# Rotating q and k with the other half of the partitions, in a kernel of windowed attention and routed experts

## Chip, cores and metric

The kernel runs on one core of a Trainium2 chip. The metric is the time of one execution on the device in microseconds (us). The engines are called as the profile calls them: PE (TensorE, matrix products), PEld (its loads of weights), DVE (VectorE), ACT (ScalarE), POOL (GpSimd), SP (SyncE, whose queue issues most of the DMAs).

## What is computed

One transformer layer over 16 batches of 256 tokens of width 128, with 16 heads of 8 dimensions. Cut to what matters here:

```python
q = (layernorm(x) @ q_w.T + q_b)            # per head: (B, H, S, 8)
k = (ctx @ k_w.T + k_b)
def apply_rope(x):                          # half = 4
    x1, x2 = x[..., :half], x[..., half:]
    return concatenate([x1 * cos - x2 * sin, x1 * sin + x2 * cos], axis=-1)
q, k = apply_rope(q) * d ** -0.5, apply_rope(k)
# each query looks at its own key and the 64 before it
probs = softmax(q . k over the window);  x = x + (probs . v) @ o_w.T + o_b
# then: layernorm, top 2 of 8 experts with limited capacity, silu(h @ w1) @ w2, weighted sum
```

A head's rotated vector needs, for each dimension, the dimension itself times a cosine and the one four further on (or back) times a sine.

## The kernel before

The work has two stages. The attention stage goes through the 16 batches in steps, each of which works on several batches at once: in step k the scores and probabilities of batch k, the maxima of batch k+1, the projections and the rotation of batch k+3, the first normalisation of batch k+4, and behind them the output of batch k-1 and the routing of batch k-2, whose rows POOL scatters to the queues of the experts in DRAM. The expert stage follows: 8 experts, three chunks of rows each.

Every engine has its program written out by hand in a fixed order (`body(k, par, pair)` for each engine, run from step -4 to 17, the middle ones in a loop), and the engines meet only at semaphores: `after(engine, name, per, batch)` waits until `name` has been raised `per` times for each batch so far. So an instruction that waits holds up all that stands behind it on its engine.

PE goes through eight units u in each step. In a unit stand the scores by key of batch k, the scores by query of batch k+1, one of the smaller jobs, and the products of the probabilities with v. The projections are such jobs (`project`): of q at u = 3 into bank m0, of k at u = 4 into bank m2. The normalised x and the context lie transposed in `xcT`, with the dimensions on the partitions. Weights are laid out with the outputs ordered by dimension: partition d * 16 + h holds dimension d of head h, so partitions 0 to 63 hold dimensions 0 to 3 of all heads and 64 to 127 dimensions 4 to 7. WQ and WK are the columns of these weights in `wts`, WQR and WKR the same with the halves exchanged. Each projection is made twice, side by side in one bank.

DVE adds the bias (a column of `cbias`) and multiplies with a table of `cst`: with cosines into `straight`, with signed sines into `turned` (`rope`, L989; i = 0 and 1). The rotation of q is in DVE's order between the pieces of the routing of batch k-2 (`diff`, `chosen`, `both`) and ahead of the sixth maximum of the step; that of k stands behind the two `xn` (L927, the normalisation of batch k+4) and ahead of the seventh maximum.

POOL adds both to `qk` (L1306). Then q and k are cut into three bf16 parts whose sum is the f32 value: ACT casts the first (L810), POOL takes the rest (L1309), ACT casts the second (L814), POOL makes the third (L1312). In POOL's order follow `rstd` of the second normalisation (L1316), four indirect DMAs to the queues (L1260), and in the next step `base` (L1292), the tags (L1293) and `rstd` of the first normalisation (L1298), for which DVE's `xn` wait, and then the next `qk`.

SP's queue takes the parts to scratch memory (L340, L345), from where q_pack and k_pack are loaded. Behind these it has the maxima: PE transposes them (L564), ACT copies them to `maxT` (L767), SP writes them out (L371) and reads them back into a row of q_pack (L378), and PE waits for that ahead of u = 0 and u = 4 of its scores by key. SP also loads `xres` (L407), which waits for `x1` (L1129), the residual sum on DVE. `masks` (L1060) are copies at the start of the program, on partitions 64 to 127, which stand right behind the rotation of k in the second and third step.

The pieces of the code that decide:

```python
cos, sin = np.cos(ang).astype(f), np.sin(ang).astype(f)
sin = np.where((np.arange(P) // HEADS < half)[:, None], -sin, sin)
...
a = np.concatenate([a[:, HD // 2:], a[:, :HD // 2]], axis=1)     # by_dim(w, turn=True)
```

Of the kernel before, what the change touches and what calls it, by code (L numbers as in the profile page):

```python
# [31 lines left out]
ALU = mybir.AluOpType  # L32
# [3 lines left out]
P = 128  # L36
BATCHES = 16
TOKENS = 256
CONTEXT = 1601
DIM = 128  # L40
# [39 lines left out]
WQ, WQR, WK, WKR, WV, WO, WR = (n * DIM for n in range(7))  # L80
# [3 lines left out]
def build(nc, x, ctx_in, weights, col_bias, row_bias, consts, consts16, q_rows, k_rows, w1, w2, out):  # L84
# [7 lines left out]
    with es:  # L92
# [12 lines left out]
        cst = sb("cst", [P, CONSTS])  # L105
        cst16 = sb("cst16", [P, 3 * P], BF16)
        wts = sb("wts", [P, WEIGHTS])
        cbias = sb("cbias", [P, 5])
# [19 lines left out]
        xcT = two("xcT", [P, 2 * TOKENS])  # L128
        straight = sb("straight", [P, 2, TOKENS])
        turned = sb("turned", [P, 2, TOKENS])  # L130
# [61 lines left out]
        S = {}  # L192
# [11 lines left out]
        def after(eng, name, per, batch, n=None):  # L204


            n = per if n is None else n
            if isinstance(batch, int):
                if batch >= BATCHES:
                    batch, n = BATCHES - 1, per  # L210
                if batch * per + n <= 0:
                    return
            eng.wait_ge(S[name], batch * per + n)
# [246 lines left out]
        def _(pe):  # L460
            def mm(o, l, r, start=True, stop=True):
                return nc.tensor.matmul(o, l, r, start=start, stop=stop)  # L462
# [9 lines left out]
            def readers(k, *waits):  # L472
                for name, per, batch, n in (waits if isinstance(k, int) else waits[-1:]):
                    after(pe, name, per, batch, n)

            def in_turn(n, this, before):


                return before[n:] + this[:n]

            def m0_read(k, n):
                readers(k, *in_turn(n, [("v_s", 1, k + 1, 1), ("norm_s", 2, k - 1, 1), ("roped_q", 2, k + 3, 2),
                                        ("ranked", 1, k - 2, 1)],
                                    [("v_s", 1, k, 1), ("norm_s", 2, k - 2, 1), ("roped_q", 2, k + 2, 2),
                                     ("ranked", 1, k - 3, 1)]))

            def m1_read(k, n):
# [3 lines left out]
                                     ("mt_s", 2, k, 1), ("ctxt_s", 1, k - 2, 1)]))  # L491

            def m2_read(k, n):
                readers(k, *in_turn(n, [("xn2t_s", 1, k - 2, 1), ("indexed", 2, k - 2, 2), ("roped_k", 2, k + 3, 2),
                                        ("x1_s", 1, k - 1, 1)],
                                    [("xn2t_s", 1, k - 3, 1), ("indexed", 2, k - 3, 2), ("roped_k", 2, k + 2, 2),
                                     ("x1_s", 1, k - 2, 1)]))

            def scores_by_query(j, par, u):
# [77 lines left out]
                        last = nc.tensor.transpose(m1[:, (2 + t) * P:(3 + t) * P], cin[1 - par][:, t, :], ident)  # L577
                    last.then_inc(S["xt_mm"], 1)

            def project(k, par, m, w, wr, cols, name, free, n):  # L580
                if on(k + 3):
                    free(k, n)
                    after(pe, "xct_s", 1, k + 3)
                    mm(m[:, 0:TOKENS], wts[:, w:w + DIM], xcT[1 - par][:, cols:cols + TOKENS])
                    mm(m[:, TOKENS:2 * TOKENS], wts[:, wr:wr + DIM], xcT[1 - par][:, cols:cols + TOKENS]
                       ).then_inc(S[name], 1)

            def context_across(k, par, t):
                j = k - 1
# [8 lines left out]
            def body(k, par, pair):  # L598
                if isinstance(k, int) and k == -1:
                    pe.wait_ge(S["obias_s"], 1)  # L600
                for u in range(UNITS):
                    scores_by_key(k, par, u)
                    if u < UNITS - 1:
                        scores_by_query(k + 1, 1 - par, u + 1)
                    else:
                        if isinstance(k, int) and -2 <= k < 0:
                            pe.wait_ge(S["masks_made"], 3 * (k + 3))
                        scores_by_query(k + 2, par, 0)
                    if u == 0:
                        values(k, par)  # L610
                        maxima_across(k, k, 1, 0)
                    if u == 1:
                        inputs_across(k, par)
                    if u == 2:
                        if on(k - 2):
                            m2_read(k, 0)
                            after(pe, "xn2_s", 2, k - 2)
                            for t in range(TILES):
                                last = nc.tensor.transpose(m2[:, t * P:(t + 1) * P], rows[par][:, 0, t, 0:DIM], ident)
                            last.then_inc(S["xn2t_mm"], 1)  # L620
                        context_across(k, par, 0)
                        context_across(k, par, 1)
                        if on(k - 2):
                            m2_read(k, 1)
                            for t in range(TILES):
                                last = mm(m2[:, t * EXPERTS:(t + 1) * EXPERTS], xn2T[:, t * P:(t + 1) * P],
                                          wts[:, WR:WR + EXPERTS])
                            last.then_inc(S["logit_mm"], 1)
                    if u == 3:
                        project(k, par, m0, WQ, WQR, 0, "q_mm", m0_read, 2)  # L630
                        maxima_across(k, k + 1, 0, 3)
                    if u == 4:
                        project(k, par, m2, WK, WKR, TOKENS, "k_mm", m2_read, 2)
                    if u == 5:
                        if on(k - 1):
                            m1_read(k, 4)
                            after(pe, "norm_s", 2, k - 1)
                            for t in range(TILES):
                                last = nc.tensor.transpose(m1[:, t * P:(t + 1) * P], ctxn[:, t, :], ident)
                            last.then_inc(S["ctxt_mm"], 1)  # L640
                        if on(k - 2):
                            m0_read(k, 3)
                            after(pe, "both_s", 1, k - 2)

                            b = both16[:].rearrange("p t e -> p (t e)")
                            mm(m0[:, 0:16], earlier16, b, True, False)
                            mm(m0[:, 8:16], ones16, b[:, 0:8], False, True)
                            mm(m0[:, 16:24], ones16, b[:, 0:8], True, False)
                            mm(m0[:, 16:24], ones16, b[:, 8:16], False, True).then_inc(S["prefix_mm"], 1)
                    if u == 6 and on(k - 1):  # L650
                        m2_read(k, 3)
                        after(pe, "ctxt_s", 1, k - 1)
                        if isinstance(k, int) and k == 1:
                            pe.wait_ge(S["bias_made"], 4)
                        mm(m2[:, 0:TOKENS], ones16[0:BIAS_ROWS, :], bias_rows[:].rearrange("p t c -> p (t c)"), True, False)
                        for t in range(TILES):
                            last = mm(m2[:, t * P:(t + 1) * P], ctxT[:, t * P:(t + 1) * P], wts[:, WO:WO + DIM], False, t == TILES - 1)
                        last.then_inc(S["y_mm"], 1)
                    if u == 0:
                        weigh_values(k - 1, 1 - par, UNITS - 1)  # L660
                    else:
                        weigh_values(k, par, u - 1)
# [210 lines left out]
        def _(dve):  # L873
            v = nc.vector
# [107 lines left out]
            def rope(k, name, mms, m, which, c0, b0, i):  # L982

                if not on(k + 3):
                    return
                if i == 0:
                    after(dve, mms, 1, k + 3)
                    after(dve, "qk_s", 1, k + 2)
                v.scalar_tensor_tensor((straight, turned)[i][:, which, :], m[:, i * TOKENS:(i + 1) * TOKENS],  # L989
                                       cbias[:, b0 + i:b0 + i + 1], cst[:, c0 + i * TOKENS:c0 + (i + 1) * TOKENS],  # L990
                                       ALU.add, ALU.mult).then_inc(S[name], 1)

            def route(k, par, n):

# [243 lines left out]
        def _(pool):  # L1238
# [48 lines left out]
            def body(k, par, pair):  # L1287
# [11 lines left out]
                if isinstance(k, int) and k == FIRST:  # L1299
                    start()  # L1300
                if on(k + 3):
                    after(pool, "roped_q", 2, k + 3)
                    after(pool, "roped_k", 2, k + 3)
                    after(pool, "part1", 1, k + 2)
                    after(pool, "rest_s", 1, k + 2)
                    g.tensor_tensor(qk[:], straight[:], turned[:], ALU.add).then_inc(S["qk_s"], 1)  # L1306
                    after(pool, "part1", 1, k + 3)
                    after(pool, "part2", 1, k + 2)
                    g.tensor_tensor(rest[:], qk[:], parts[:, 0, :, :], ALU.subtract).then_inc(S["rest_s"], 1)  # L1309
# [102 lines left out]
```

## Time and profile before

| | us |
|---|---|
| median of 3 runs | 570.44 (567.39 to 571.85) |
| profiled execution | 574.74 |
| its span, first to last instruction | 572.7 |
| filling the pipeline, 0 to 129.4 us of the span | 129.4 |
| attention, 129.4 to 246.3 us | 116.9 |
| last batches, routing and scatter, 246.3 to 358 us | 111.7 |
| experts, 358 us to the end | about 215 |

In the stretch from 129.4 to 246.3 us PE is busy 105.5 us, DVE 99.5, ACT 63.8 and POOL 84.4, at a granted clock of 1.00; in the expert stage PE is busy 148.9 of 215 us and POOL 139.6. A busy share says what an engine has to do, not that the others wait for it: for that one reads the gaps, what ended them, and the chain of the work that ended last. PE's busy time is modelled from the starts of its instructions, since matrix products overlap; each f32 product has two records. On POOL neighbouring records overlap too, and where the profile puts a gap down to "issue" it knows of no instruction that ended it.

### The profile page before, as it was taken

Reading aid. Unit: us, or ns where it says so; the run is one execution under the profiler, and the core shown is the slowest. Engines: PE = TensorE matmul, PEld = TensorE weight load, DVE = VectorE, ACT = ScalarE, POOL = GpSimd, SP = SyncE. Lnnn points to the kernel's source line nnn. Section 1 sums busy time; section 2 is a strip of 40 time slices with the busy share of each in tenths; the row PEclk is TensorE's granted clock in tenths of the full one; section 3 lists DMA queues with packets and bytes.
Section 4 is the critical chain, followed back from the end, with each engine's and each line's share of the span. In section 5 each row is a group of like instructions: output and inputs, shape, how many; then the busy total and the mean of one; then the engine's idle time right before and its main releaser. Section 6 shows DMA issues by size and latency. Waiting matters only on the chain.

```text
span 572.7 us, 16559 instructions
## 1 busy us (share of the span) xinstructions
PE 410.8 (72%) x5570; PEld 321.5 (56%) x5570; DVE 345.2 (60%) x1055; ACT 262.9 (46%) x578; POOL 344.1 (60%) x289
## 2 busy tenths in 40 slices
PE   3373598779988999788869830499978769879300
PEld 2252466657766776666657620378867658668200
DVE  4783376757988888868766652177635636545200
ACT  1111255435654555444444620289847748557100
POOL 6432023357776777765664677007787687787874
PEclk9995788999999999989988975599989989888855
DMA  9895766577877888876875335524554554432432
GB/s 184 210 242 146 174 191 171 148 161 164 193 155 172 184 183 174 166 163 148 153 156 106 43 51 77 138 83 67 108 83 64 106 83 60 78 32 25 36 28 18
DMA packets 89615, 70.50 MB, mean 123 GB/s; under 512 B 9632, under 2 KB 76448, under 8 KB 89056
## 3 DMA queue, kind: packets, MB, share of 16 engines
q1 hardware_dynamic: 68576, 60.36, 41.2%
q0 software_dynamic: 20992, 9.53, 19.3%
q8 instruction: 28, 0.46, 0.4%
q14 instruction: 19, 0.16, 0.1%
HBM read 39.11 MB, written 31.00 MB: 122 GB/s over the span
## 4 chain that ended last, share of the span: by engine, by line
POOL 25%; issue 18%; DMA 7%; PE 6%; SPq 3%; DVE 1%; ACT 1%; POOLq 0%; ACTq 0%; DVEq 0%
POOL out L1336 16%; POOL queues L1260 6%; PE bank L462 5%; DMA out<-ys,row_token 3%; DMA maxima_scratch<-maxT 1%; SPq L345 1%; SPq L340 1%; DMA q_pack<-maxima_scratch 1%; DMA xs<-queues 1%; POOL base L1292 1%; POOL parts L1312 1%; POOL rest L1309 1%; DMA queues<-rows,index 1%; PE bank L681 0%; ACT parts L810 0%
## 5 line engine op out<-in xcount | busy, mean ns | idle before, releaser
L1336 POOL DMA_INDIRECT out<-ys,row_token x88 | 138.8, 1578 | 68.4 <-DVE ys L1195 31.3
L885 DVE TENSOR_REDUCE maxima<-bank 128x4 f32<-128x512 f32 x128 | 87.3, 685 | 63.8 <-PE bank L462 60.6
L1260 POOL DMA_INDIRECT queues<-rows,index x64 | 100.6, 1571 | 19.8 <-issue 19.1
L753 ACT ACTIVATE probs<-bank 128x512 f32<-128x512 f32 x128 | 76.4, 597 | 78.3 <-PE bank L462 77.8
L462 PE MATMUL bank<-xTp,w1p 128*128 128x512 f32 (+1 forms) x288 | 71.6, 403 | 13.4 <-DVE xTp L1146 13.4
L462 PE MATMUL bank<-q_pack,k_pack 128*128 128x64 bf16 x1024 | 54.9, 199 | 34.3 <-DMA q_pack<-maxima_scratch 32.8
L462 PEld LDWEIGHTS bank<-xTp,w1p 128*128 128x128 f32 x288 | 53.8, 213 | 25.4 <-issue 8.3
L856 ACT ACTIVATE hid<-bank 128x512 f32<-128x512 f32 (+1 forms) x96 | 53.7, 559 | 29.6 <-PE bank L462 28.4
L462 PE MATMUL bank<-k_pack,q_pack 128*64 128x128 bf16 x1024 | 56.1, 236 | 15.6 <-DMA k_pack<-k_scratch 15.6
L462 PEld LDWEIGHTS bank<-q_pack,k_pack 128*128 128x128 bf16 x1024 | 39.1, 101 | 48.6 <-DMA q_pack<-maxima_scratch 32.5
L462 PE MATMUL bank<-probs,v_sb 128*32 128x64 f32 x2048 | 57.6, 231 | 7.8 <-ACT csb L760 4.9
L1218 DVE TENSOR_TENSOR hidp<-hid,hidp 128x512 fp32r<-128x512 f32 (+1 forms) x96 | 55.4, 601 | 12.4 <-ACT hidp L860 11.5
L462 PE MATMUL bank<-hidp,w2p 128*128 128x512 f32 (+1 forms) x288 | 61.7, 363 | 0.5 <-DVE hidp L1218 0.5
L1195 DVE TENSOR_TENSOR ys<-bank,row_gate 128x512 f32<-128x512 f32 (+1 forms) x24 | 14.4, 602 | 75.6 <-DMA out<-ys,row_token 74.6
L1306 POOL TENSOR_TENSOR qk<-straight,turned 128x512 f32<-128x512 f32 x16 | 22.2, 1390 | 58.1 <-DVE turned L989 37.9
L860 ACT ACTIVATE hidp<-bank 128x512 fp32r<-128x512 f32 (+1 forms) x96 | 54.2, 564 | 0.0
L462 PEld LDWEIGHTS bank<-hidp,w2p 128*128 128x128 f32 x288 | 46.8, 188 | 7.8 <-issue 0.8
L462 PEld LDWEIGHTS bank<-probs,v_sb 128*32 128x32 f32 x2048 | 36.5, 112 | 21.7 <-issue 12.6
L462 PEld LDWEIGHTS bank<-k_pack,q_pack 128*64 128x64 bf16 x1024 | 34.9, 116 | 24.1 <-issue 8.1
L462 PE MATMUL bank<-xcT,wts 128*128 128x256 f32 x128 | 42.9, 469 | 5.7 <-ACT xcT L784 5.7
L462 PEld LDWEIGHTS bank<-xcT,wts 128*128 128x128 f32 x128 | 25.9, 223 | 12.3 <-issue 5.9
L1298 POOL TENSOR_TENSOR rstd<-var,half_neg 128x2 f32<-128x2 f32 x16 | 16.0, 997 | 26.3 <-DVE var L922 26.2
(113 smaller groups left out, 664.6 us busy)
## 6 DMA issues: line engine op xcount, KB each, us to landing
k_pack<-k_scratch SPq DMA_DIRECT2D x64, 192.0 KB, 3.9
q_pack<-q_scratch SPq DMA_DIRECT2D x64, 128.0 KB, 3.2
queues<-empty SPq DMA_DIRECT2D x8, 682.5 KB, 7.3
xs<-queues SPq DMA_DIRECT2D x8, 650.0 KB
q_scratch<-parts SPq DMA_DIRECT2D x16, 192.0 KB
k_scratch<-parts SPq DMA_DIRECT2D x16, 192.0 KB
xin<-in_x SPq DMA_DIRECT2D x16, 128.0 KB, 3.2
cin<-in_ctx SPq DMA_DIRECT2D x16, 128.0 KB, 3.4
```

Of the source, the lines that this page charges most:

```text
L340: sp.dma_start(to[:, at:at + times, :], parts[:, part, 0, :].unsqueeze(1).to_broadcast([P, times, TOKENS])).then_inc(S["scr_w"], 16)
L462: return nc.tensor.matmul(o, l, r, start=start, stop=stop)
L753: nc.scalar.activation(probs[u % 2][:], bb[u % 2][:], ACT.Exp).then_inc(S["prob_s"], 1)
L856: nc.scalar.activation(hid[s][:, f, 0:CHUNKS[c]], up[f][:, 0:CHUNKS[c]], ACT.Silu).then_inc(S["silu_s"], 1)
L860: nc.scalar.activation(hidp[s][:, 0, f, 0:CHUNKS[c]], up[f][:, 0:CHUNKS[c]], ACT.Silu).then_inc(S["h_hi"], 1)
L885: v.reduce_max(maxima[par][:, 4 * hg:4 * hg + 4, i2], ab[u % 2][:].rearrange("p (h c) -> p h c", c=P), AX).then_inc(S["max_s"], 1)
L1195: ins = v.tensor_tensor(ys[s][:, 0:m, :], yt[:, 0:m * DIM].rearrange("p (t c) -> p t c", c=DIM), row_gate[par][:, t0:t0 + m].unsqueeze(2). ...
L1218: v.tensor_tensor(hidp[s][:, 1, f, 0:CHUNKS[c]], hid[s][:, f, 0:CHUNKS[c]], hidp[s][:, 0, f, 0:CHUNKS[c]].bitcast(F32), ALU.subtract).then ...
L1260: g.indirect_dma_start(queues, bass.IndirectOffsetOnAxis(ap=index[par][:, n:n + 1], axis=0), rows[par][:, n // TILES, n % TILES, :], None, ...
L1298: g.tensor_tensor(rstd1[:], var1[:], half_neg[:], ALU.pow).then_inc(S["rstd1_s"], 1)
L1306: g.tensor_tensor(qk[:], straight[:], turned[:], ALU.add).then_inc(S["qk_s"], 1)
L1336: g.indirect_dma_start(out, bass.IndirectOffsetOnAxis(ap=row_token[par][0:n, t:t + 1], axis=0), ys[s][0:n, col // P, :], None, compute_op= ...
```

## The change

The projections with exchanged weights go. `project` makes one product of 128x256 for q and one for k. `straight` is made as before. `turned` is made by two instructions on 64 partitions each: partitions 0 to 63 of `turned` from partitions 64 to 127 of the projection, and the other way round; bias column and table of sines are read on the partitions that are written. `roped_q` and `roped_k` are raised three times in a batch instead of twice, and those who wait for them wait for three. The columns WQR and WKR are still loaded with the weights.

```diff
@@ PE: project, and its two calls
-            def project(k, par, m, w, wr, cols, name, free, n):
+            def project(k, par, m, w, cols, name, free, n):
                 if on(k + 3):
                     free(k, n)
                     after(pe, "xct_s", 1, k + 3)
-                    mm(m[:, 0:TOKENS], wts[:, w:w + DIM], xcT[1 - par][:, cols:cols + TOKENS])
-                    mm(m[:, TOKENS:2 * TOKENS], wts[:, wr:wr + DIM], xcT[1 - par][:, cols:cols + TOKENS]
-                       ).then_inc(S[name], 1)
+                    mm(m[:, 0:TOKENS], wts[:, w:w + DIM], xcT[1 - par][:, cols:cols + TOKENS]).then_inc(S[name], 1)
@@ DVE: rope
-                v.scalar_tensor_tensor((straight, turned)[i][:, which, :], m[:, i * TOKENS:(i + 1) * TOKENS],
-                                       cbias[:, b0 + i:b0 + i + 1], cst[:, c0 + i * TOKENS:c0 + (i + 1) * TOKENS],
-                                       ALU.add, ALU.mult).then_inc(S[name], 1)
+                if i == 0:
+                    v.scalar_tensor_tensor(straight[:, which, :], m[:, 0:TOKENS], cbias[:, b0:b0 + 1],
+                                           cst[:, c0:c0 + TOKENS], ALU.add, ALU.mult).then_inc(S[name], 1)
+                else:
+                    for here, there in ((slice(0, P // 2), slice(P // 2, P)), (slice(P // 2, P), slice(0, P // 2))):
+                        v.scalar_tensor_tensor(turned[here, which, :], m[there, 0:TOKENS], cbias[here, b0 + 1:b0 + 2],
+                                               cst[here, c0 + TOKENS:c0 + 2 * TOKENS], ALU.add, ALU.mult
+                                               ).then_inc(S[name], 1)
@@ POOL: ahead of qk (PE's waits for its banks m0 and m2 alike)
-                    after(pool, "roped_q", 2, k + 3)
-                    after(pool, "roped_k", 2, k + 3)
+                    after(pool, "roped_q", 3, k + 3)
+                    after(pool, "roped_k", 3, k + 3)
```

In DVE's order of a middle step before, from the rotation of q (first straight and turned) to that of k and the maximum behind it:

```order
L989 SCALAR_TENSOR_TENSOR straight<-bank,cbias,cst 128x256
L1021 TENSOR_TENSOR diff<-top 128x2
L1023 TENSOR_TENSOR chosen<-cst,top_index 128x32
L989 SCALAR_TENSOR_TENSOR turned<-bank,cbias,cst 128x256
L1030 TENSOR_TENSOR both<-chosen 128x16
L885 TENSOR_REDUCE maxima<-bank 128x4
L927 TENSOR_SCALAR xn<-xin,mv,rstd 128x128 x2
L989 SCALAR_TENSOR_TENSOR straight<-bank,cbias,cst 128x256
L989 SCALAR_TENSOR_TENSOR turned<-bank,cbias,cst 128x256
L885 TENSOR_REDUCE maxima<-bank 128x4
```

The same place now:

```order
L988 SCALAR_TENSOR_TENSOR straight<-bank,cbias,cst 128x256
L1024 TENSOR_TENSOR diff<-top 128x2
L1026 TENSOR_TENSOR chosen<-cst,top_index 128x32
L992 SCALAR_TENSOR_TENSOR turned<-bank,cbias,cst 64x256 x2
L1033 TENSOR_TENSOR both<-chosen 128x16
L883 TENSOR_REDUCE maxima<-bank 128x4
L925 TENSOR_SCALAR xn<-xin,mv,rstd 128x128 x2
L988 SCALAR_TENSOR_TENSOR straight<-bank,cbias,cst 128x256
L992 SCALAR_TENSOR_TENSOR turned<-bank,cbias,cst 64x256 x2
L883 TENSOR_REDUCE maxima<-bank 128x4
```

Nothing has moved; each turned has become two of 64 partitions, at the place of the one.

In PE's order of a middle step before, from u = 3 (the projection of q) to u = 4 (that of k); q_pack and k_pack are the scores, max_parts the transposed maxima:

```order
L462 MATMUL bank<-xcT,wts 128x256 x2
L564 MATMUL bank<-cst,max_parts 32x128
L462 MATMUL bank<-probs,v_sb 32x64 x8
L462 MATMUL bank<-q_pack,k_pack 128x64 x8
L462 MATMUL bank<-k_pack,q_pack 64x128 x8
L462 MATMUL bank<-xcT,wts 128x256 x2
```

The same place now:

```order
L462 MATMUL bank<-xcT,wts 128x256
L564 MATMUL bank<-cst,max_parts 32x128
L462 MATMUL bank<-probs,v_sb 32x64 x8
L462 MATMUL bank<-q_pack,k_pack 128x64 x8
L462 MATMUL bank<-k_pack,q_pack 64x128 x8
L462 MATMUL bank<-xcT,wts 128x256
```

One product stands where two stood, and all else keeps its place.

## Rows read from the trace of the kernel before

**Rows 1.** The page: busy time by engine; chain that ended last.
```profile
PE 410.8 (72%) x5570; PEld 321.5 (56%) x5570; DVE 345.2 (60%) x1055; ACT 262.9 (46%) x578; POOL 344.1 (60%) x289
...
POOL 25%; issue 18%; DMA 7%; PE 6%; SPq 3%; DVE 1%; ACT 1%; POOLq 0%; ACTq 0%; DVEq 0%
```

**Rows 2.** Timeline of POOL: start, us, engine, line, form [idle before, releaser].
```profile
196.73 1.27 POOL L1306 TENSOR_TENSOR qk<-straight,turned 128x512 f32<-128x512 f32 x1 [1.56 <-issue]
198.80 1.16 POOL L1309 TENSOR_TENSOR rest<-qk,parts 128x512 f32<-128x512 f32 x1 [0.81 <-ACT parts L810]
...
202.86 1.59 POOL L1260 DMA_INDIRECT queues<-rows,index  x1 [0.21 <-issue]
...
210.25 1.28 POOL L1298 TENSOR_TENSOR rstd<-var,half_neg 128x2 f32<-128x2 f32 x1
213.09 1.27 POOL L1306 TENSOR_TENSOR qk<-straight,turned 128x512 f32<-128x512 f32 x1 [1.56 <-issue]
```

**Rows 3.** Timeline of DVE in the same step, 193 to 197 us.
```profile
193.72 0.47 DVE L989 SCALAR_TENSOR_TENSOR turned<-bank,cbias,cst 128x256 f32<-128x256 f32 x1
...
194.31 0.68 DVE L885 TENSOR_REDUCE maxima<-bank 128x4 f32<-128x512 f32 x1
195.20 0.60 DVE L927 TENSOR_SCALAR xn<-xin,mv,rstd 128x128 f32<-128x128 f32 x2 [0.22 <-POOL rstd L1298]
195.72 0.48 DVE L989 SCALAR_TENSOR_TENSOR straight<-bank,cbias,cst 128x256 f32<-128x256 f32 x1
196.11 0.47 DVE L989 SCALAR_TENSOR_TENSOR turned<-bank,cbias,cst 128x256 f32<-128x256 f32 x1
196.51 0.68 DVE L885 TENSOR_REDUCE maxima<-bank 128x4 f32<-128x512 f32 x1
```

**Rows 4.** Timeline of POOL: first and last qk of the stretch, and the next.
```profile
143.78 1.28 POOL L1298 TENSOR_TENSOR rstd<-var,half_neg 128x2 f32<-128x2 f32 x1
146.80 1.26 POOL L1306 TENSOR_TENSOR qk<-straight,turned 128x512 f32<-128x512 f32 x1 [1.75 <-issue]
...
246.33 1.27 POOL L1306 TENSOR_TENSOR qk<-straight,turned 128x512 f32<-128x512 f32 x1 [2.02 <-issue]
...
266.02 1.27 POOL L1306 TENSOR_TENSOR qk<-straight,turned 128x512 f32<-128x512 f32 x1 [4.63 <-DVE turned L989]
```

**Rows 5.** Timeline of DVE: copies on partitions 64 to 127 behind the rotation.
```profile
26.87 0.47 DVE L989 SCALAR_TENSOR_TENSOR turned<-bank,cbias,cst 128x256 f32<-128x256 f32 x1
27.38 1.22 DVE L1060 COPY q_pack<-mask_rows 64x4096 bf16<-64x4096 bf16 x1
28.52 4.38 DVE L1060 COPY k_pack<-mask_rows 64x4096 bf16<-64x4096 bf16 x2
```

**Rows 6.** All instructions of DVE by form: few partitions against many.
```profile
L1199 DVE TENSOR_TENSOR ys<-bank,row_gate 4x128 f32<-4x128 f32 x8 | 2.1, 269 | 0.0
...
L1065 DVE TENSOR_TENSOR rbias<-rbias,bank 128x128 f32<-128x128 f32 x1 | 0.3, 286 | 0.7 <-PE bank L462 0.7
```

**Rows 7.** Timeline of DVE ahead of that first qk, 144 to 147 us.
```profile
145.30 0.59 DVE L927 TENSOR_SCALAR xn<-xin,mv,rstd 128x128 f32<-128x128 f32 x2
```

**Rows 8.** Timeline of PE, the projection of q, and where PE next stands.
```profile
190.97 1.13 PE L462 MATMUL bank<-xcT,wts 128*128 128x256 f32 x4
...
192.97 0.41 PE L462 MATMUL bank<-q_pack,k_pack 128*128 128x64 bf16 x8 [0.49 <-DMA q_pack<-maxima_scratch]
```

**Rows 9.** Who waited for whom, 73 to 147 us: SyncE's queue, then DVE.
```profile
SPq L378 <- DMA maxima_scratch<-maxT: 9.6, 6, 3.3
...
DVE straight L989 <- PE bank L462: 1.6, 3, 0.8
```

**Rows 10.** Chain that ended last, 246 to 268 us: start, us, what.
```profile
250.42 0.40 SPq L407
...
267.65 0.62 ACT parts L810
```

**Rows 11.** Busy us of PE, PEld, DVE, ACT, POOL (counts); clock; DMA share; GB/s.
```profile
196.50:213.00 16.50, 15.42 (x325) 12.00 (x315) 14.30 (x53) 9.38 (x22) 12.04 (x11) 1.00 0.84 180
```

More of the change, by code:

```diff
@@ L481, in m0_read @@
             def m0_read(k, n):
-                readers(k, *in_turn(n, [("v_s", 1, k + 1, 1), ("norm_s", 2, k - 1, 1), ("roped_q", 2, k + 3, 2),
+                readers(k, *in_turn(n, [("v_s", 1, k + 1, 1), ("norm_s", 2, k - 1, 1), ("roped_q", 3, k + 3, 3),
                                         ("ranked", 1, k - 2, 1)],
-                                    [("v_s", 1, k, 1), ("norm_s", 2, k - 2, 1), ("roped_q", 2, k + 2, 2),
+                                    [("v_s", 1, k, 1), ("norm_s", 2, k - 2, 1), ("roped_q", 3, k + 2, 3),
                                      ("ranked", 1, k - 3, 1)]))
@@ L493, in m2_read @@
             def m2_read(k, n):
-                readers(k, *in_turn(n, [("xn2t_s", 1, k - 2, 1), ("indexed", 2, k - 2, 2), ("roped_k", 2, k + 3, 2),
+                readers(k, *in_turn(n, [("xn2t_s", 1, k - 2, 1), ("indexed", 2, k - 2, 2), ("roped_k", 3, k + 3, 3),
                                         ("x1_s", 1, k - 1, 1)],
-                                    [("xn2t_s", 1, k - 3, 1), ("indexed", 2, k - 3, 2), ("roped_k", 2, k + 2, 2),
+                                    [("xn2t_s", 1, k - 3, 1), ("indexed", 2, k - 3, 2), ("roped_k", 3, k + 2, 3),
                                      ("x1_s", 1, k - 2, 1)]))
@@ L629, in body @@
                     if u == 3:
-                        project(k, par, m0, WQ, WQR, 0, "q_mm", m0_read, 2)
+                        project(k, par, m0, WQ, 0, "q_mm", m0_read, 2)
                         maxima_across(k, k + 1, 0, 3)
                     if u == 4:
-                        project(k, par, m2, WK, WKR, TOKENS, "k_mm", m2_read, 2)
+                        project(k, par, m2, WK, TOKENS, "k_mm", m2_read, 2)
                     if u == 5:
```

## The prediction

> **What bounds the kernel now.** I read the page first. POOL holds 25% of the chain that ended last, the largest share of any engine, while PE, the busiest by the clock (72%), holds 6% [rows 1]. So the projections that go are work of an engine that is busy and seldom last. Those shares don't add up to the whole, since that chain can't be followed back to the start; the steps before it have to be read from the timelines.
>
> In the timeline of POOL from 146.80 to 246.33 us the steps lie 99.53 us apart in six periods, 16.59 us each [rows 4]; the undisturbed one is 16.36 us, from a qk at 196.73 to the next at 213.09 [rows 2]. Nearly every gap in it has its cause inside the step: qk, rest and the third part with ACT's two casts between them, rstd, four scatters from 202.86 on, base, the tags, rstd again until 211.53 (210.25 + 1.28), and then 1.56 us of idleness before the next qk. The profile calls that gap "issue", and this is where it misleads: in the same place one step earlier DVE starts its two xn at 195.20, 0.06 us behind POOL's rstd, has straight of k at 195.72 and turned of k from 196.11 to 196.58, and POOL's qk starts at 196.73 [rows 2, 3]. So the loop runs POOL, DVE (xn, straight, turned), POOL, and **the rotation of k is a link of it**. Everything that this rotation grows by, each period grows by.
>
> The other engines follow this loop. Behind the projection of q PE stands idle 0.49 us for the maxima of the second half of the heads [rows 8], which SyncE's queue brings only after it has taken the three parts of q and k from POOL.
>
> **What goes.** Two of the four 128x256 projections of a step. Four records of PE take 1.13 us, so one projection of q less is 0.57 us, one of k the same, 1.13 us a step and 18 us of PE's time in 16 batches, at the full clock. In the locked stretch I give it nothing: behind the projection of q PE comes to its wait of 0.49 us for the DMA of the maxima, and arrives there earlier to wait longer [rows 8]; behind that of k the next such wait is at the head of the following step. Where DVE's straight waits for PE it is worth something: three times between 73 and 147 us, 1.6 us in all [rows 9]. What hides it there is SyncE's queue, which in the same steps waits 9.6 us for the maxima to land in DRAM and paces the loads behind it [rows 9]; and the halves of the rotation take back what the earlier projection gives (below). Zero for these steps, with up to 1.6 us of gain in the range.
>
> **What comes.** Two DVE instructions on 64 partitions in place of one on 128, for q and for k, 32 more in all; POOL waits for three signals of each instead of two, which costs nothing by itself. First the duration. A DVE operation on 4x128 takes 269 ns and one on 128x128 286 ns [rows 6]: fewer partitions save nothing, and each half will take the 0.47 us that turned takes now.
>
> Then the distance between two of them. Where neighbours use the same partitions, the second starts before the first has ended: straight to turned 0.39 us, turned to maxima 0.40 us, with durations of 0.47 [rows 3]. The halves read and write other partitions than their neighbours. The nearest rows are the mask copies, on partitions 64 to 127: the first starts at 27.38, 0.51 us behind the start of turned and 0.04 behind its end, though nothing is waited for; the next, on the same partitions as the first, starts 1.14 behind a start of 1.22, so 0.08 us before the end [rows 5]. I take 0.51 for every change of partitions: straight to first half, first to second, second to whatever follows.
>
> The Trainium skill, in "VectorE: DVE Perf Modes", section "Two Vector instructions with no wait between them", says that an instruction whose first input or output starts in another group of 32 partitions than the last one's in that memory begins only when all earlier ones have finished. By that rule the halves and the operation behind them are all held, and the trace agrees at the mask copies.
>
> For the rotation of k, from the start of straight to the signal of the last half: 0.39 + 0.47 = 0.86 us before, 0.51 + 0.51 + 0.47 = 1.49 after, **+0.63 us on the loop**. DVE itself is occupied for 3 x 0.51 = 1.53 instead of 0.39 + 0.40, so +0.75 for each of q and k. If there is no hold, both are +0.39.
>
> For the rotation of q: its turned stands at 193.72, ahead of maxima and xn, where DVE waits 0.22 us for POOL's rstd [rows 3]. Of +0.75, 0.53 would stick out in a first such period. But DVE's work there hangs on loads that SyncE starts from the parts of the step before, so when the period grows by 0.63, DVE is that much earlier against POOL, and 0.22 + 0.63 covers 0.75. I take zero for q in the locked periods, 0.53 at the other end. At the entry of the stretch there is no such cover: xn starts at 145.30 with no idleness before it, 0.24 us behind the end of POOL's rstd (143.78 + 1.28) [rows 4, 7]. So the qk of 146.80 comes 0.75 + 0.63 = 1.38 later.
>
> **The sum.** Entry +1.38. Five periods, up to the qk before the last one of the stretch, from which the later chain starts, at +0.63: +3.15. The periods that were longer than 16.36 (99.53 - 6 x 16.36 = 1.37 us in all) were so because a load came late; a later POOL forgives part of that, I take off a third, 0.5. Behind 246 us the chain leaves POOL's loop and runs by SyncE's queue and PE: x is released by DVE, 250.42 is SyncE's load that waits for x, and at 267.65 ACT's first part waits for its own turn [rows 10]. DVE reaches that x about 0.6 us later, and the qk of that last stretch comes 0.63 later against a slack of 0.36 (it ends at 267.29, 266.02 + 1.27 [rows 4], and the part starts at 267.65), +0.3 more. PE's savings there go into those same waits. Sum 1.38 + 3.15 - 0.5 + 0.6 + 0.3 = 4.9, say **+5 us**. The expert stage has none of the changed code. The profiled execution took 574.74 us (span 572.7, and 2.0 around it), so 579.7 on its own scale. It lies 4.3 above the median of 570.44, and I carry the difference over: 575.4 us. With the alternatives in the same mechanism (no forgiveness, or all of it; gains of up to 1.6 before 147 us) it spans 573 to 577.
>
> **Rivals.**
> (1) *No hold*: the halves follow at 0.39 like all neighbours now. Entry 0.78, five periods 1.95, less 0.5, behind 246 us 0.5: +2.7, 573.1 us. For it: 64-partition copies that go from SBUF to SBUF are the only rows of a hold, and the halves read PSUM. Against it: the hold is seen without any wait.
> (2) *DVE becomes the bound.* DVE is busy 14.30 of 16.5 us in a locked step [rows 11]; with 1.5 more it is at 15.8 of 17. If its remaining waits for PE and POOL (0.22 and what PE causes) don't give way, q's half is on the loop too, and each period grows by 0.63 + 0.53, up to 1.5: 1.38 + 5 x 1.16 to 5 x 1.5 and 1.5 behind it, +8.7 to +10.4, 580 us, slower by over 1.5%. It decides once DVE comes to xn later than POOL's rstd ends in the undisturbed periods; now it is 0.22 early.
> (3) *PE's time is worth something.* If PE's relief moves the maxima of the first half forward, and with them SyncE's loads, the 1.6 us of straight's waits and 0.57 in two of the last stretches come back, and the rotation is no worse than in (1): 2.7 - 1.6 - 1.1 = 0, or, if POOL's loop takes up slack that I don't see, down to -2.5: 568 to 570.4. Against it are the 0.15 us between the end of turned and qk, which show the rotation, not PE, in front of POOL [rows 2, 3].
> (4) *The edit is not what it says*: three signals with one late would stall POOL. The halves follow each other on DVE with nothing in between, so I give this nothing beyond (2).
>
> **How the numbers follow.** Chances: forecast 0.47, (1) 0.23, (2) 0.17, (3) 0.13. One per cent, 5.7 us, is about what a measurement of this kernel can tell from no change (the three runs of before span 4.5). Over +5.7: all of (2) and a good third of the forecast, 0.17 + 0.17 = 0.34. Under -5.7: a tail of (3), 0.03. Within: 0.63. The range leaves out the lower third of (3) and the upper end of (2): 569.0 to 580.5.
>
> **What the changed profile would show.** Right: half as many records of PE on xcT and wts at 128x256; 64 turned instructions of about 0.47 us, each 0.51 behind the start in front; qk 2.2 us behind rstd's end instead of 1.56; an undisturbed period of 17.0 us. Periods of 16.75 speak for (1), of 17.5 and more for (2), with xn behind its rstd. The expert stage should take as long as before. I am wrong if the halves are shorter than 0.47 us, or if periods stay at 16.4.

## The result, and the profile after

Median 574.44 us in 17 runs (570.87 to 578.31) against 570.67 us in as many runs of before (567.09 to 576.88). The ratio is 1.0082, 95% interval 1.0058 to 1.0105: slower by 4.7 us, with 3.3 to 6.0 in the interval. The profiled execution has a span of 571.9 us, 0.8 *less* than that of before. One profiled execution can't settle a difference of 0.8%; below I show which parts of it repeat and which scatter.

The page, with the span, the busy times, and the shares of the chain that ended last:

```profile
span 571.9 us, 16479 instructions
...
PE 407.4 (71%) x5506; PEld 316.9 (55%) x5506; DVE 359.5 (63%) x1087; ACT 263.3 (46%) x578; POOL 344.6 (60%) x289
...
POOL 25%; issue 17%; DMA 7%; PE 7%; SPq 2%; ACT 1%; DVE 1%; POOLq 0%; ACTq 0%; DVEq 0%
```

DVE has 14.3 us more to do than in [rows 1], about what 32 instructions at 0.48 make (15.4). PE's busy time is only 3.4 us less: the row below is 14.6 less than before, and records of other rows came out longer, at a mean granted clock of 0.873 against 0.887 of before. The chain is led by POOL as before. The line of the page for the projections, and the answer for the halves (duration in ns, lowest, median, highest):

```profile
L462 PE MATMUL bank<-xcT,wts 128*128 128x256 f32 x64 | 28.3, 540 | 5.4 <-ACT xcT L782 5.4
```

```profile
L992 DVE SCALAR_TENSOR_TENSOR turned<-bank,cbias,cst x64: 479/482/486, 12.5 to 284.3; 64x256 f32<-64x256 f32 x64
```

64 records instead of 128, and 64 halves at 482 ns each: half the partitions take as long as all of them did (0.47 us in [rows 3]). The timeline of DVE in a locked step, to be laid beside [rows 3]:

```profile
191.40 0.69 DVE L883 TENSOR_REDUCE maxima<-bank 128x4 f32<-128x512 f32 x1
193.35 0.60 DVE L925 TENSOR_SCALAR xn<-xin,mv,rstd 128x128 f32<-128x128 f32 x2 [1.25 <-POOL rstd L1301]
193.87 0.47 DVE L988 SCALAR_TENSOR_TENSOR straight<-bank,cbias,cst 128x256 f32<-128x256 f32 x1
194.37 1.00 DVE L992 SCALAR_TENSOR_TENSOR turned<-bank,cbias,cst 64x256 f32<-64x256 f32 x2
195.40 0.69 DVE L883 TENSOR_REDUCE maxima<-bank 128x4 f32<-128x512 f32 x1
```

straight starts at 193.87, the first half 0.50 behind it, and the two halves together take 1.00 with 0.48 for one, so the second starts about 0.52 behind the first; maxima starts 1.03 behind the first half and 0.03 behind the end of the second. All three starts are held until the instruction in front has ended, where [rows 3] has 0.39 and 0.40. From the start of straight to the end of the last half it is 1.50 us. The timeline of POOL, which answers to [rows 2, 4]:

```profile
144.40 1.27 POOL L1309 TENSOR_TENSOR qk<-straight,turned 128x512 f32<-128x512 f32 x1 [2.20 <-issue]
...
192.03 1.28 POOL L1301 TENSOR_TENSOR rstd<-var,half_neg 128x2 f32<-128x2 f32 x1
195.51 1.27 POOL L1309 TENSOR_TENSOR qk<-straight,turned 128x512 f32<-128x512 f32 x1 [2.20 <-issue]
...
212.53 1.27 POOL L1309 TENSOR_TENSOR qk<-straight,turned 128x512 f32<-128x512 f32 x1 [2.20 <-issue]
...
247.27 1.27 POOL L1309 TENSOR_TENSOR qk<-straight,turned 128x512 f32<-128x512 f32 x1 [2.88 <-issue]
```

The gap ahead of qk is 2.20 instead of 1.56 us, and the undisturbed period 17.02 instead of 16.36. The six periods from 144.40 to 247.27 are 102.87 us, 3.34 more than the 99.53 of before. The waits of that stretch, 146 to 230 us, DVE and then PE (in total, times, longest):

```profile
DVE xn L925 <- POOL rstd L1301: 5.7, 5, 1.4
DVE maxima L883 <- PE bank L462: 1.4, 5, 0.3
...
PE bank L462 <- DMA q_pack<-maxima_scratch: 7.0, 6, 1.5
PE bank L462 <- DVE turned L992: 2.6, 3, 1.1
```

DVE is not late for xn: with q's halves in front of it, it still waits there in all five steps (5.7 us, 0.8 to 1.4 each). PE has a new wait, for the halves themselves. PE's timeline has it at one place, in three of the five steps:

```profile
161.37 0.28 PE L462 MATMUL bank<-bias_rows,cst 96*128 96x256 bf16 x1 [1.06 <-DVE turned L992]
```

This is the start of the output of batch k-1, which goes into m2, the bank that the rotation of k reads. Behind it PE goes on to wait for the maxima, as before. The last two qk of the program:

```profile
267.57 1.27 POOL L1309 TENSOR_TENSOR qk<-straight,turned 128x512 f32<-128x512 f32 x1 [4.41 <-issue]
...
284.96 1.26 POOL L1309 TENSOR_TENSOR qk<-straight,turned 128x512 f32<-128x512 f32 x1 [2.21 <-issue]
```

From 247.27 to 284.96 are 37.69 us, against 37.02 before (246.33 [rows 4] to 283.35 in the same timeline): 0.67 more.

### The profile page after: what moved, and what is told of

It reads as the page before. It is cut to its first block, busy times and chain, and to the rows that moved or that the text cites. A ratio compares the mean times of both kernels' runs of the same rounds, so it can differ in the third digit from the quotient of the medians.

```text
span 571.9 us, 16479 instructions
## 1 busy us (share of the span) xinstructions
PE 407.4 (71%) x5506; PEld 316.9 (55%) x5506; DVE 359.5 (63%) x1087; ACT 263.3 (46%) x578; POOL 344.6 (60%) x289
## 4 chain that ended last, share of the span: by engine, by line
POOL 25%; issue 17%; DMA 7%; PE 7%; SPq 2%; ACT 1%; DVE 1%; POOLq 0%; ACTq 0%; DVEq 0%
POOL out L1339 16%; POOL queues L1263 6%; PE bank L462 6%; DMA out<-ys,row_token 3%; DMA maxima_scratch<-maxT 2%; SPq L345 1%; DMA q_pack<-maxima_scratch 1%; SPq L340 1%; POOL rest L1312 1%; POOL parts L1315 1%; POOL base L1295 1%; DMA xs<-queues 1%; DMA queues<-rows,index 1%; PE bank L679 0%; ACT parts L808 0%
## 5 line engine op out<-in xcount | busy, mean ns | idle before, releaser
L462 PE MATMUL bank<-q_pack,k_pack 128*128 128x64 bf16 x1024 | 56.2, 202 | 36.2 <-DMA q_pack<-maxima_scratch 35.6
L462 PE MATMUL bank<-xTp,w1p 128*128 128x512 f32 (+1 forms) x288 | 73.3, 411 | 12.2 <-DVE xTp L1149 12.1
L462 PE MATMUL bank<-k_pack,q_pack 128*64 128x128 bf16 x1024 | 58.5, 244 | 17.5 <-DMA k_pack<-k_scratch 15.4
L462 PEld LDWEIGHTS bank<-xTp,w1p 128*128 128x128 f32 x288 | 55.0, 217 | 24.7 <-issue 7.9
L462 PEld LDWEIGHTS bank<-q_pack,k_pack 128*128 128x128 bf16 x1024 | 40.3, 102 | 50.5 <-DMA q_pack<-maxima_scratch 36.3
L1221 DVE TENSOR_TENSOR hidp<-hid,hidp 128x512 fp32r<-128x512 f32 (+1 forms) x96 | 55.3, 600 | 12.2 <-ACT hidp L858 11.5
L462 PE MATMUL bank<-probs,v_sb 128*32 128x64 f32 x2048 | 58.9, 235 | 5.7 <-ACT csb L758 4.1
L462 PEld LDWEIGHTS bank<-k_pack,q_pack 128*64 128x64 bf16 x1024 | 36.5, 120 | 27.3 <-issue 15.7
L992 DVE SCALAR_TENSOR_TENSOR turned<-bank,cbias,cst 64x256 f32<-64x256 f32 x64 | 30.9, 483 | 2.1
L462 PE MATMUL bank<-xcT,wts 128*128 128x256 f32 x64 | 28.3, 540 | 5.4 <-ACT xcT L782 5.4
```

The costliest lines, as they stand in the source:

```text
L992: v.scalar_tensor_tensor(turned[here, which, :], m[there, 0:TOKENS], cbias[here, b0 + 1:b0 + 2], cst[here, c0 + TOKENS:c0 + 2 * TOKENS], A ...
L1221: v.tensor_tensor(hidp[s][:, 1, f, 0:CHUNKS[c]], hid[s][:, f, 0:CHUNKS[c]], hidp[s][:, 0, f, 0:CHUNKS[c]].bitcast(F32), ALU.subtract).then ...
```

## Experiments

Each kernel was timed beside the kernel before, on the same chip as that. "Period" is the undisturbed one, and "six periods" the time between the eighth and the fourteenth qk of the program, both from the timeline of POOL of each profile.

| kernel | ratio to before (95%) | period, us | six periods, us |
|---|---|---|---|
| before | 1 | 16.36 | 99.53 |
| changed kernel | 1.0082 (1.0058 to 1.0105) | 17.02 | 102.87 |
| only k changed | 1.0023 (0.9988 to 1.0058) | 17.00 | 102.47 |
| only q changed | 1.0013 (0.9977 to 1.0048) | 16.37 | 99.57 |
| halves, both projections kept | 1.0063 (1.0031 to 1.0096) | 17.01 | 102.85 |
| projections alone | 0.9965 (0.9939 to 0.9991) | 16.38 | 98.51 |
| two instructions, same partitions | 1.0013 (0.9984 to 1.0042) | 16.75 | 101.62 |
| changed, k's rotation ahead of xn | 1.0044 (1.0003 to 1.0084) | 16.99 | 103.90 |
| before, k's rotation ahead of xn | 0.9985 (0.9953 to 1.0016) | 16.61 | 100.36 |
| changed, xn last as well | 1.0041 (1.0001 to 1.0081) | none | 100.26 |
| before, xn last as well | 1.0008 (0.9966 to 1.005) | none | 98.40 |

**Only k.** One projection and two halves for k; q as before (waits for roped_q count two, for roped_k three).

```diff
+                if which == 1:      # k as in the changed kernel: straight, two halves
...
+                else:               # q as before: two projections, one turned
```

> Only k is changed (one projection, two halves); q keeps its two projections and its one turned. Theory (k's rotation is a link of POOL's loop, q's is hidden): the undisturbed period between two qk is 17.0 us as in the changed kernel, time 3.5 to 5 us over before. Rival (DVE's total work, or PE's, sets the period): half of the effect, period near 16.7, time 2 to 2.5 us over before.

POOL's timeline, two qk in a row:

```profile
180.45 1.27 POOL L1319 TENSOR_TENSOR qk<-straight,turned 128x512 f32<-128x512 f32 x1 [2.14 <-DVE turned L998]
...
197.45 1.27 POOL L1319 TENSOR_TENSOR qk<-straight,turned 128x512 f32<-128x512 f32 x1 [2.14 <-DVE turned L998]
```

17.00 us apart, with a gap of 2.14. The period is that of the changed kernel, so k alone makes it. The time is 1.3 us over before with an interval from -0.7 to +3.3; it doesn't reach the 3.5 to 5 that I expected. The six periods are 2.94 us longer in its profile, which the interval allows; that they come back whole in the time is not shown.

**Only q.** The same with the roles exchanged.

```diff
+                if which == 0:      # q as in the changed kernel: straight, two halves
...
+                else:               # k as before
```

> Only q is changed; k keeps its two projections and its one turned. Theory: period 16.36 us or up to 0.53 more where DVE now reaches xn behind POOL's rstd (no growth of the period from k that would hide q's 0.75), time 0 to +3 us. Rival (the work as such counts): half of the effect, +2.4 us. If the lever is PE: below before, -0.5 to -1.5 us.

POOL's timeline:

```profile
196.56 1.27 POOL L1319 TENSOR_TENSOR qk<-straight,turned 128x512 f32<-128x512 f32 x1 [1.56 <-issue]
...
212.93 1.27 POOL L1319 TENSOR_TENSOR qk<-straight,turned 128x512 f32<-128x512 f32 x1 [1.56 <-issue]
```

16.37 us apart: q's halves do nothing to the undisturbed period, and the six are 99.57 us. DVE's timeline at the entry of the stretch:

```profile
143.75 1.00 DVE L998 SCALAR_TENSOR_TENSOR turned<-bank,cbias,cst 64x256 f32<-64x256 f32 x2
...
145.48 0.59 DVE L930 TENSOR_SCALAR xn<-xin,mv,rstd 128x128 f32<-128x128 f32 x2
```

The halves start at 143.75, xn at 145.48 with no idleness in front of it, so DVE comes to xn late there, 0.42 us behind the end of rstd (143.78 + 1.28 on POOL) against 0.24 in before. The period that ends with this qk, at 146.99, is 18.27 us long against 17.37 in before, +0.90; but only 0.18 of that stands between rstd and qk (1.93 us against 1.75). The rest lies at the head of the period, which POOL's timeline shows in this kernel, and then in before:

```profile
128.72 1.27 POOL L1319 TENSOR_TENSOR qk<-straight,turned 128x512 f32<-128x512 f32 x1 [3.40 <-issue]
132.31 1.17 POOL L1322 TENSOR_TENSOR rest<-qk,parts 128x512 f32<-128x512 f32 x1 [2.32 <-ACT parts L813]
```

```profile
129.43 1.28 POOL L1306 TENSOR_TENSOR qk<-straight,turned 128x512 f32<-128x512 f32 x1 [5.25 <-issue]
132.29 1.17 POOL L1309 TENSOR_TENSOR rest<-qk,parts 128x512 f32<-128x512 f32 x1 [1.58 <-ACT parts L810]
```

The qk in front came 0.71 us earlier, and then POOL waited for ACT until the same time. So q costs nothing once the loop is locked, and 0.2 us where DVE is behind when it enters. Where DVE is behind again, in the last period of the stretch, the gap is 2.40 us against 2.02. From there to the last qk this profile has 39.15 us against 37.02 of before; one profile can't say whether q's halves make that.

**Halves without the saving.** Both projections stay on PE, the second is made and not read.

```diff
-                    mm(m[:, 0:TOKENS], wts[:, w:w + DIM], xcT[1 - par][:, cols:cols + TOKENS]).then_inc(S[name], 1)
+                    mm(m[:, 0:TOKENS], wts[:, w:w + DIM], xcT[1 - par][:, cols:cols + TOKENS])
+                    mm(m[:, TOKENS:2 * TOKENS], wts[:, w + DIM:w + 2 * DIM], xcT[1 - par][:, cols:cols + TOKENS]
+                       ).then_inc(S[name], 1)
```

> Both projections stay on PE as before (the second is made and not read), the rotation is made in halves from the first. Theory: PE's saving is worth nothing, so the time is that of the changed kernel within 1 us (+0.8% on before) and the period 17.0 us. Rival (PE's saving was worth something and hid part of the cost): 1.5 to 3 us slower than the changed kernel.

```profile
180.55 1.27 POOL L1311 TENSOR_TENSOR qk<-straight,turned 128x512 f32<-128x512 f32 x1 [2.19 <-issue]
...
197.62 1.27 POOL L1311 TENSOR_TENSOR qk<-straight,turned 128x512 f32<-128x512 f32 x1 [2.20 <-issue]
```

These two qk are 17.07 us apart (the next 17.01) and six periods take 102.85 us, within 0.02 of the changed kernel; the ratio, 1.0063, is within its interval. With the halves in place, the projections that go (18 us of PE by my count) buy nothing that the periods or the time can show. The clock of PE is no rival for the period either: from 129 to 247 us this kernel ran at a granted clock of 1.00, as before did, and the changed one at 0.95.

**The saving without the halves.** One projection, and turned made by one instruction of 128 partitions from the same columns. It leaves out the exchange of the halves, so its output is another one.

```diff
-                v.scalar_tensor_tensor((straight, turned)[i][:, which, :], m[:, i * TOKENS:(i + 1) * TOKENS],
+                v.scalar_tensor_tensor((straight, turned)[i][:, which, :], m[:, 0:TOKENS],
```

> Only the projections go: turned is made by one instruction of 128 partitions from the one projection without exchanging the halves, so the output differs. Theory: the 1.13 us of PE per step are hidden, period 16.36 us, time within 1 us of before. Rival: the saving is worth 1.5 to 3 us and the kernel is faster than before by as much.

```profile
176.16 1.27 POOL L1304 TENSOR_TENSOR qk<-straight,turned 128x512 f32<-128x512 f32 x1 [1.56 <-issue]
...
192.58 1.27 POOL L1304 TENSOR_TENSOR qk<-straight,turned 128x512 f32<-128x512 f32 x1 [1.56 <-issue]
```

The period stays, but here none is longer than 16.48, where before has three of 16.66 to 16.85: six periods take 98.51 us, 1.02 less. The ratio is 0.9965 (0.9939 to 0.9991), 2.0 us faster, with 0.5 to 3.5 in the interval, and not within 1 us as I expected. So PE's saving seems to be worth something by itself, and the profile has a place for half of it, the long periods that are gone. But this profile takes as long as before's from the seventh qk to the last (153.79 us against 153.92): the 1.02 us come back behind the stretch. Where the time goes down is not shown. In the changed kernel POOL's longer loop takes up the slack of the long periods anyway, which is why the two experiments needn't add up.

**Two instructions without a change of partitions.** Each half is an instruction on all 128 partitions from the same partitions, the second into a spare tile, so the halves aren't exchanged and the output is another one.

```diff
-                    for here, there in ((slice(0, P // 2), slice(P // 2, P)), (slice(P // 2, P), slice(0, P // 2))):
-                        v.scalar_tensor_tensor(turned[here, which, :], m[there, 0:TOKENS], cbias[here, b0 + 1:b0 + 2],
-                                               cst[here, c0 + TOKENS:c0 + 2 * TOKENS], ALU.add, ALU.mult
+                    for to in (turned, turned2):
+                        v.scalar_tensor_tensor(to[:, which, :], m[:, 0:TOKENS], cbias[:, b0 + 1:b0 + 2],
+                                               cst[:, c0 + TOKENS:c0 + 2 * TOKENS], ALU.add, ALU.mult
                                                ).then_inc(S[name], 1)
```

> The changed kernel, but each half is an instruction on all 128 partitions from the same partitions (the second goes into a spare tile; the halves are not exchanged, so the output differs). As many instructions as in the changed kernel, but no change of partitions between neighbours. Theory (the hold at a change of partitions costs 0.12 us each time): starts 0.39 to 0.40 us apart, from straight to the last signal 1.25 us, period 16.36 + 0.39 = 16.75 us, time 1.5 to 2.5 us under the changed kernel. Rival (what costs is the signal or the read of the other half, not the start partition): starts 0.51 apart, period 17.0, time as the changed kernel.

DVE's timeline:

```profile
194.22 0.60 DVE L926 TENSOR_SCALAR xn<-xin,mv,rstd 128x128 f32<-128x128 f32 x2 [1.23 <-POOL rstd L1302]
194.74 0.48 DVE L989 SCALAR_TENSOR_TENSOR straight<-bank,cbias,cst 128x256 f32<-128x256 f32 x1
195.13 0.87 DVE L993 SCALAR_TENSOR_TENSOR turned<-bank,cbias,cst 128x256 f32<-128x256 f32 x2
195.92 0.68 DVE L884 TENSOR_REDUCE maxima<-bank 128x4 f32<-128x512 f32 x1
```

Now straight to the first is 0.39 us, the two take 0.87 (0.40 + 0.47), and maxima starts 0.79 behind the first. The period is 16.75 to 16.81: of the 0.66 us that the change adds to a period, 0.39 to 0.45 is the second instruction and 0.21 to 0.27 the hold at the two changes of partition on the path. In time it is 1.0013, below the changed kernel's 1.0082 with intervals that don't meet; the 3.9 us between them are more than the 1.5 to 2.5 that I expected and than the 1.25 us by which the six periods differ, and I have no row for the rest.

**k's rotation ahead of xn**, in the changed kernel and in that of before. If the rotation is a link only because it stands behind xn, which waits for POOL, this takes it out.

```diff
-                norm1(k, par, 3)
...
                 rope(k, "roped_k", "k_mm", m2, 1, COSK, 2, 0)
                 rope(k, "roped_k", "k_mm", m2, 1, COSK, 2, 1)
+                norm1(k, par, 3)
```

> The changed kernel with k's rotation ahead of xn in DVE's order. Theory (loop POOL rstd, DVE xn, straight, turned, POOL qk): k's rotation then hangs on PE and the maxima, which leave DVE idle 0.8 to 1.4 us ahead of xn; DVE starts it about 1 us earlier, the gap between rstd and qk falls from 2.2 us to 1.0 or less, period 16.0 us or less where another link comes last (SyncE's queue and the maxima's DMA), time 4 to 9 us under the changed kernel. Rival (DVE's whole work or SyncE sets the period): no change beyond 1 us, or slower since xn comes later.

> The kernel before with k's rotation ahead of xn. Theory: DVE waits only 0.22 us ahead of xn and the two projections of k end later than in the changed kernel, so the rotation starts 0.2 to 0.5 us earlier at most; then qk no longer waits for xn (0.5 us), gap 1.56 falls to 0.7 to 1.0, period 15.6 to 16.1 us, time 2 to 6 us under before. Against the changed kernel with the same order it shows what the change costs once the rotation is off POOL's loop: within 1.5 us. Rival: no change beyond 1 us.

Both misses: 1.0044 and 0.9985, periods of 16.99 and about 16.6. POOL's timeline of the first shows the gap closed and another opened:

```profile
163.88 1.37 POOL L1309 TENSOR_TENSOR qk<-straight,turned 128x512 f32<-128x512 f32 x1
...
171.11 0.70 POOL L1319 TENSOR_TENSOR rstd<-var,half_neg 128x2 f32<-128x2 f32 x1 [1.98 <-DVE var L948]
...
179.42 1.29 POOL L1301 TENSOR_TENSOR rstd<-var,half_neg 128x2 f32<-128x2 f32 x1
180.87 1.37 POOL L1309 TENSOR_TENSOR qk<-straight,turned 128x512 f32<-128x512 f32 x1 [0.16 <-issue]
```

qk now follows rstd at once in five of the seven steps from 146 to 251 us (0.17 us of gap at most; the other two have 2.05, and one of them ends a period of 18.97), but the second rstd waits 1.98 us for var of DVE. And DVE's timeline shows why var is late:

```profile
179.74 1.00 DVE L992 SCALAR_TENSOR_TENSOR turned<-bank,cbias,cst 64x256 f32<-64x256 f32 x2
180.77 1.55 DVE L925 TENSOR_SCALAR xn<-xin,mv,rstd 128x128 f32<-128x128 f32 x2
182.24 0.68 DVE L883 TENSOR_REDUCE maxima<-bank 128x4 f32<-128x512 f32 x1
```

The two xn take 1.55 us where they took 0.60; they end at 182.32, and POOL's qk, which started at 180.87, ends at 182.24. It is so in each step of both kernels of this order from 160 to 244 us (1.54 to 1.58 us). The rotation came off one loop and xn went onto another: rstd of POOL, xn, DVE's work down to var, second rstd, the scatters. In the changed kernel it happens to be as long (16.99 against 17.02 us), in that of before it is 0.25 longer.

**xn last**: the same, and xn moved behind var, to the end of DVE's step, which cuts this loop too.

```diff
                 norm2(k, par, 2)
+                norm1(k, par, 3)
             steps(dve, body)
```

> The changed kernel with k's rotation where xn stood and xn at the very end of DVE's step. Theory after the run with k's rotation first: there the loop only moved, to POOL rstd, DVE xn (held up by POOL's qk), DVE's work up to var, POOL's second rstd, which waited 2.0 us for var. With xn behind var this loop is cut too, POOL no longer waits 2.0 us there, and the period falls below 16.4 us to where SyncE or PE comes last, about 15.5 to 16.2; time 3 to 9 us under the changed kernel. Rival (DVE's whole work, 15.8 of 17 us, is the bound by now): period 16.5 to 17.0 and no gain.

> The kernel before with the same order. Theory: as above, period 15.3 to 16.0 us, 3 to 8 us under before; against the changed kernel in this order it shows what the exchange by halves costs once neither rotation nor xn is in POOL's loop: 0 to 1.5 us. Rival: period 16.4, no gain.

POOL's waits for var are gone, and there is no steady period any more, 15.6 to 17.3 us in the changed kernel and 15.8 to 17.0 in that of before. Who is waited for in the changed kernel, 146 to 247 us, PE and then SyncE's queue:

```profile
PE bank L462 <- DMA q_pack<-maxima_scratch: 11.5, 9, 2.5
...
SPq L378 <- DMA maxima_scratch<-maxT: 15.0, 9, 3.3
```

PE now waits 11.5 us for the way of the maxima through DRAM, where with k's rotation first the same answer has no such wait, and SyncE's queue waits 15.0 us for their landing against 6.6 there. That this way bounds the period is my reading and not shown: the kernel with the projections alone has 11.5 and 13.6 us of the same waits at a period of 16.38. Six periods take 100.26 and 98.40 us, 2.6 and 1.1 less than in the old order, but both expectations of the time miss: neither kernel is measurably faster than before (1.0041 and 1.0008, both intervals hold 1.001). No order of either kernel beats before beyond its interval.

## Why the prediction was right

*The link.* "The rotation of k is a link of it": shown. Only k gives the whole growth of the period (17.00 us), only q gives none (16.37). One reading was off by little: xn starts 0.04 us behind the end of POOL's rstd (193.86 + 1.30, and 195.20), not 0.06.

*+0.63 us on the loop.* Measured 0.66 (17.02 against 16.36). The duration of a half was taken at 0.47 and came as 0.48, and all three changes of partition were held at 0.50 to 0.52. With the changes of partition taken out, the growth is 0.39 to 0.45, the value that I gave to the case of no hold.

*The Trainium skill's rule* ("VectorE: DVE Perf Modes", "Two Vector instructions with no wait between them"), by which an instruction is held until all earlier ones have finished when its first input or its output starts in another group of 32 partitions than the last one's in that memory, agrees with the three starts here (0.50 to 0.52 us, and maxima 1.03 behind the first half); the run with equal partitions, at 0.39 and 0.40, is its counterpart.

*q at zero in the locked periods.* Right, and by more than I had reckoned: DVE waits 0.8 to 1.4 us ahead of xn in the changed kernel, where I had 0.1 of cover left (0.22 + 0.63 - 0.75). In the kernel where only q is changed, the period doesn't grow by 0.63, and yet it stays at 16.37; so q's cover wasn't the growth of the period. That step of the reasoning was wrong though its result was right.

*Entry +1.38.* This is the term that was off. In the profile of the changed kernel the period into the stretch is 17.02 us against 17.37 of before, so there is no extra at all; DVE waits 1.16 us for POOL's rstd there. Where only q is changed, xn is late there, but by 0.18 us more than in before where I had 0.75: its halves start at 143.75, and turned in before at 144.22. Over the seven kernels in the old order the gap ahead of this qk is longer than the locked one in three, those with both projections of k (before, only q, halves with both projections), and the locked one in the four that make k's projection once. That is one profile of each, and no experiment was made for it; but it points at PE's saving for k, which lets DVE come to xn in time there and which I had put at nothing in the sum.

*Five periods +3.15, less 0.5 forgiven.* 85.18 us from 144.40 to 229.58 against 82.71 before, +2.47 where I had 2.65. All five lie between 17.01 and 17.05, so the late loads were forgiven entirely. A sixth came to 17.69 against 16.82, +0.87, which I had counted to what lies behind.

*+0.9 behind 246 us.* In the profile 0.67. That tests the term hardly at all: from the fourteenth qk to the last the seven profiles in the old order have 37.0 to 39.2 us, with 39.2 where only q is changed and 38.0 where only the projections go.

*PE's saving at zero.* Right in the locked periods of the changed kernel (halves with and without it: 102.85 and 102.87), and probably not at the entry (above). Alone it measured 2.0 us (0.5 to 3.5), so it may be hidden by what came with it and not worthless in itself; as far as that holds, rival (3) had a true part.

*The sum.* From the seventh qk to the last the profile of after takes 157.58 us (127.38 to 284.96) and that of before 153.92 (129.43 to 283.35): +3.7, where my terms gave 4.9. By terms it is -0.35 at the entry (I had +1.38), +2.47 and +0.87 in the periods and +0.67 behind them. The measured 4.7 is 1.0 more than that. The rest, ahead of the seventh qk and behind the last, is 2.0 and 2.4 us *shorter* in the profile of after. Over the eleven profiles of this study the seventh qk comes between 125.9 and 129.5 us and the stretch behind the last qk takes 282.1 to 289.4, with no order by kernel, so single profiles can't tell where that last microsecond is. It stays open. The link and the cost of a period were right; that the total of 5 met 4.7 so closely is in part luck, since terms that gave 1.2 us too much (the entry above all) stood in for 1.0 us that none of them has. It stays open too why only k (1.0023) plus only q (1.0013) stay below both together (1.0082), and why the kernel with two instructions on equal partitions shows 1.0013 with six periods that are 2.09 us longer; the intervals of the single ones are 0.6 to 0.7% wide, and neither needs a cause beyond them.

*Rival (2)*, DVE as the bound, fell: DVE waits more for POOL than before, not less.

## What to carry to other kernels

When an engine's idle gap in front of an instruction is the same in every step and the profile names no cause, look on the other engines for the chain that fits into it exactly; here what stood in that chain cost its full length each step, and work of a busier engine outside it didn't change the undisturbed period. Trading a matrix product for one more vector instruction is a bad trade when the vector engine is in the loop, and splitting an instruction by partitions cost it whole a second time (0.48 us for each half, 0.47 for the whole), plus 0.12 us at every change of partitions. And a link that is taken out of a loop by reordering has to be followed to where its neighbour goes: here the changed kernel had a period of 17.02 us in one order and 16.99 in the other.

## What the runs showed of the hardware

The hold at a change of partitions was also seen where only the read from PSUM changes: the first half writes partitions 0 to 63 as straight does and reads 64 to 127 of the bank, and it starts 0.50 us behind straight, against 0.39 for equal partitions, with durations of 0.48 and 0.47. Where input and output change, 0.52. Two xn from SBUF took 1.55 us instead of 0.60 while POOL's addition of two SBUF tiles ran, and ended 0.08 us behind it. The rotation, with one tensor from PSUM and one from SBUF, kept its 0.47 us beside POOL's base, which also reads two SBUF tiles (turned from 193.72 to 194.19 in before, base from 193.07 to 194.34).
